# Graph network on one core: 48 slots for gathered tiles in four passes, and edge results stored by pairs of groups

## The reference, cut to what matters

```
# block 0, three layers
f = einsum(x @ fc_w[l].T + fc_b[l], norm_out, ch_w[l])
agg = segment_sum(f[src] * edge_w, dst)          # a weighted sum
# block 1
out = segment_max(relu(theta(x[dst] - x[src]) + phi(x[src])), dst)
# block 2: attention over edges and self loops
# block 3, three layers
e = relu((x[dst] - x[src]) @ thetas[l].T + x[src] @ phis[l].T)
agg = segment_max(e, src); batch norm; relu
```

## Time and profile before

| what | value |
|---|---|
| median of 3 executions | 4967.33 us |
| the profiled execution's own time | 4953.19 us |
| its span, first to last instruction | 4951.5 us |
| POOL busy | 3314.2 us (67%), 3435 instructions |
| DVE busy | 3038.7 us (61%), 9035 instructions |
| PE busy | 1527.9 us (31%) |
| ACT busy | 1032.0 us (21%) |
| gathers of line 1287 | 2744, busy 1510.6 us and 1146.0 us |
| stores of line 1270 | 686 of 512 KB, 3.2 us to landing |
| mean DMA rate | 181 GB/s |

### The profile page before, as it was taken

One profiled execution on the slowest core, in us unless ns is written; L12 is line 12 of the kernel. 1 busy time (PEld: TensorE's weight loads), 2 busy tenths in 40 slices (PEclk: granted clock), 3 DMA queues, 4 the chain that ended last, 5 costly groups with the idle time before them and its releaser, 6 DMA issues. The chain is left out here.

```text
span 4951.5 us, 34938 instructions
## 1 busy us (share of the span) xinstructions
PE 1527.9 (31%) x7148; PEld 1041.6 (21%) x7148; DVE 3038.7 (61%) x9035; ACT 1032.0 (21%) x2614; POOL 3314.2 (67%) x3435
## 2 busy tenths in 40 slices
PE   6221075556655565445520001400006000330004
PEld 5110053334433343112320001300005000230003
DVE  5897565556656568999868888633334333433335
ACT  3333334443344432000121111200002000110002
POOL 3777747776577755777657774177775777657774
PEclk8555575555655578875665555755558555665556
DMA  2766636665466634666446664166654666456663
GB/s 86 230 195 222 209 122 207 209 206 178 149 210 206 210 106 134 205 204 205 150 131 222 218 220 141 59 205 205 206 191 138 204 204 206 152 177 204 204 207 118
DMA packets 319655, 898.09 MB, mean 181 GB/s; under 512 B 75371, under 2 KB 111576, under 8 KB 319320
## 3 DMA queue, kind: packets, MB, share of 16 engines
q0 software_dynamic: 161760, 439.40, 31.9%
q1 hardware_dynamic: 157688, 456.53, 24.7%
HBM read 449.86 MB, written 445.80 MB: 181 GB/s over the span
## 5 line engine op out<-in xcount | busy, mean ns | idle before, releaser
L1287 POOL DMA_INDIRECT WORK<-table,SRCI x1568 | 1510.6, 963 | 640.0 <-issue 512.9
L1287 POOL DMA_INDIRECT WORK<-table,BYSRC x1176 | 1146.0, 975 | 559.1 <-issue 435.5
L1336 DVE SCALAR_TENSOR_TENSOR WORK<-WORK,LOWE 128x256 f32<-128x256 f32 x1564 | 763.3, 488 | 964.7 <-DMA WORK<-table,BYSRC 892.8
L1336 DVE SCALAR_TENSOR_TENSOR WORK<-WORK,NST,e_mv 128x256 f32<-128x256 f32 x1173 | 563.2, 480 | 499.7 <-ACT e_mv L1306 261.0
L1306 ACT ACTIVATE e_mv<-WORK,WE 128x256 f32<-128x256 f32 x1176 | 491.3, 463 | 826.7 <-DMA WORK<-table,SRCI 788.1
L990 PE MATMUL bn_ps<-ident,WORK 128*128 128x128 f32 x6 | 2.0, 434 | 1490.0 <-PEq L148 1490.0
L1641 POOL DMA_INDIRECT WORK<-table_attention,SRCI x392 | 373.5, 953 | 119.4 <-issue 118.8
L990 PEld LDWEIGHTS bn_ps<-ident,WORK 128*128 128x128 f32 x6 | 0.9, 203 | 1491.1 <-issue 1491.1
L1418 ACT ACTIVATE WORK<-bn_ps 128x256 f32<-128x256 f32 x3 | 1.2, 384 | 1495.2 <-PE bn_ps L1001 1495.2
L961 PE MATMUL e_hi<-ARENA 128*128 128x392 bf16 x392 | 185.1, 472 | 262.4 <-DVE ARENA L947 262.4
L897 PE MATMUL e_rb<-ARENA 98*128 98x128 bf16 x392 | 114.7, 293 | 443.5 <-ACT ARENA L913 443.5
(11 more groups left out here) (355 smaller groups left out, 4379.9 us busy)
## 6 DMA issues: line engine op xcount, KB each, us to landing
edge_results<-WORK SPq DMA_DIRECT2D x686, 512.0 KB, 3.2
edge_results_attention<-WORK SPq DMA_DIRECT2D x98, 544.0 KB, 3.2
WORK<-table,SRCI POOLq DMA_INDIRECT x1568, 2.9
table<-ARENA SPq DMA_DIRECT2D x35, 640.0 KB, 3.2
WORK<-table,BYSRC POOLq DMA_INDIRECT x1176, 2.9
WORK<-table_attention,SRCI POOLq DMA_INDIRECT x392, 3.2
table_attention<-ARENA SPq DMA_DIRECT2D x5, 660.0 KB, 3.4
X<-in_x SPq DMA_DIRECT2D x4, 640.0 KB
```

The lines of the kernel that those rows point to most:

```text
L1287: eng.indirect_dma_start(G[:, q * GT + k, 0:D], None, T, bass.IndirectOffsetOnAxis(ap=index[:, t:t + 1], axis=0)).then_inc(got[q].sem, 16)
L1336: eng.scalar_tensor_tensor(O[:, q % OB, k, :], behind, mask[:, ds(g * GT + k, 1)], here, op0, op1).then_inc(linked, 1)
```

## The change

It does two things in `edge_pass`.

1. In the four passes for a maximum (e3, e5, e6, e7) there are twelve sets of four slots in place of six, 48 in all. The new 24 lie in `AGW_BASE`. POOL there waits, before the gathers of group g, for group g - 12 in place of g - 6. Twelve semaphores count landed gathers in place of six. The weighted passes keep 24 slots.
2. In all seven passes SP stores after every odd group only, two groups (8 KB from every partition, 1024 KB) at once. There are 343 stores in place of 686. The ring of four groups stays; DVE waits before every even group g for the store of groups g - 4 and g - 3, which is issued after group g - 3. At the end SP waits for two counts in place of four.

```diff
--- before.py
+++ after.py
@@ -21,6 +21,7 @@
 GT = 4
 NG = -(-E // (P * GT))
 SETS = 6
+DEEP = 2 * SETS
 ET = NG * GT
 EP = ET * P
 CHAIN = ET
@@ -152,7 +153,7 @@
     top = ExitStack()
     Stage.used = []
     with top:
-        gathered = [Gathered(top.enter_context(nc.semaphore(f"gathered_{k}"))) for k in range(SETS)]
+        gathered = [Gathered(top.enter_context(nc.semaphore(f"gathered_{k}"))) for k in range(DEEP)]
         def sb(name, shape, dt=F32):
             return top.enter_context(nc.sbuf_tensor(name, shape, dt))
 
@@ -1249,10 +1250,18 @@
         def edge_pass(name, index, ops, mask, weighted, beside=nothing_beside):
 
             op0, op1 = ops
-            U = 2 * SETS
+            sets = SETS if weighted else DEEP
+            U = 2 * sets
+            more, = carve(AGW_BASE, ((SETS * GT, D), F32))
+
+            def slot(g, k):
+
+                at = g % sets * GT + k
+                return G[:, at, 0:D] if at < SETS * GT else more[:, at - SETS * GT, :]
+
             with Stage(nc, name) as st:
-                got = gathered
-                stored = [st.sem(f"stored{b}") for b in range(OB)]
+                got = gathered[0:sets]
+                stored = [st.sem(f"stored{b}") for b in range(OB // 2)]
                 moved, linked = (st.sem(n) for n in ("moved", "linked"))
                 mv = st.stack.enter_context(nc.psum_tensor(f"{name}_mv", [P, 4, 2 * D], F32))
                 side = beside(st, name)
@@ -1266,25 +1275,28 @@
                 @block.sync
                 def _(eng):
                     def store(g, q, turn):
-                        eng.wait_ge(linked, g * GT + (GT + 8))
-                        eng.dma_start(PRC[:, ds(g * GT, GT), :], O[:, q % OB, :, :]).then_inc(stored[q % OB], 16)
+
+                        if g % 2:
+                            eng.wait_ge(linked, g * GT + (GT + 8))
+                            pair = O[:, g % OB - 1:g % OB + 1, :, :].rearrange("p g k d -> p (g k) d")
+                            eng.dma_start(PRC[:, (g - 1) * GT:(g + 1) * GT, :], pair).then_inc(stored[g % OB // 2], 16)
 
                     early, late = beside_on("sync", eng)
                     pipelined(NG, U, eng, *early, (store, 0), *late, flat=flat)
-                    for b in range(OB):
-                        eng.wait_ge(stored[b], 16 * -(-(NG - b) // OB))
+                    for b in range(OB // 2):
+                        eng.wait_ge(stored[b], 16 * -(-(NG // 2 - b) // (OB // 2)))
 
                 @block.gpsimd
                 def _(eng):
                     for g in range(NG):
-                        q = g % SETS
-                        if g >= SETS and weighted:
-                            eng.wait_ge(moved, 2 * (g - SETS + 1))
-                        elif g >= SETS:
-                            eng.wait_ge(linked, GT * (g - SETS + 1) + 8)
+                        q = g % sets
+                        if g >= sets and weighted:
+                            eng.wait_ge(moved, 2 * (g - sets + 1))
+                        elif g >= sets:
+                            eng.wait_ge(linked, GT * (g - sets + 1) + 8)
                         for k in range(GT):
                             t = g * GT + k
-                            eng.indirect_dma_start(G[:, q * GT + k, 0:D], None, T,
+                            eng.indirect_dma_start(slot(g, k), None, T,
                                                    bass.IndirectOffsetOnAxis(ap=index[:, t:t + 1], axis=0)).then_inc(got[q].sem, 16)
 
                 @block.tensor
@@ -1298,12 +1310,12 @@
                 @block.scalar
                 def _(eng):
                     def move(g, q, turn):
-                        got[q % SETS].arrived(eng, turn * (U // SETS * GT) + (q // SETS * GT + GT))
+                        got[g % sets].arrived(eng, g // sets * GT + GT)
                         for h in range(2):
                             eng.wait_ge(linked, g * GT + (2 * h + 2))
-                            bank, first = mv[:, 2 * (q % 2) + h, :], q % SETS * GT + 2 * h
+                            bank = mv[:, 2 * (q % 2) + h, :]
                             for k in range(2):
-                                last = eng.activation(bank[:, k * D:(k + 1) * D], G[:, first + k, 0:D], ACT.Copy,
+                                last = eng.activation(bank[:, k * D:(k + 1) * D], slot(g, 2 * h + k), ACT.Copy,
                                                       scale=WE[:, ds(g * GT + (2 * h + k), 1)])
                             last.then_inc(moved, 1)
 
@@ -1318,12 +1330,12 @@
 
                     def link(g, q, turn):
                         for k in range(GT):
-                            if k == 0 and not (isinstance(g, int) and g < OB):
-                                eng.wait_ge(stored[q % OB], turn * (U // OB * 16) + q // OB * 16)
+                            if k == 0 and g >= OB and g % 2 == 0:
+                                eng.wait_ge(stored[g % OB // 2], g // OB * 16)
                             if not weighted:
                                 if k == 0:
-                                    got[q % SETS].arrived(eng, turn * (U // SETS * GT) + (q // SETS * GT + GT))
-                                here = G[:, q % SETS * GT + k, 0:D]
+                                    got[g % sets].arrived(eng, g // sets * GT + GT)
+                                here = slot(g, k)
                             else:
                                 if k % 2 == 0:
                                     eng.wait_ge(moved, g * 2 + (k // 2 + 1))
@@ -1339,8 +1351,8 @@
                     pipelined(NG, U, eng, *early, (link, 0), *late, flat=flat, head=0 if flat else U)
                     if "vector_end" in side:
                         side["vector_end"](eng)
-            for q in range(SETS):
-                got[q].close(GT * ((NG - q + SETS - 1) // SETS))
+            for q in range(sets):
+                got[q].close(GT * ((NG - q + sets - 1) // sets))
 
 
         YT = YBASE[:, 0:2 * NP].rearrange("p (k n) -> p k n", k=2)
@@ -1602,7 +1614,7 @@
 
             U = SETS
             with Stage(nc, "att") as st:
-                got = gathered
+                got = gathered[0:SETS]
                 stored = [st.sem(f"stored{b}") for b in range(OB)]
                 names = ("raw_in", "first", "er_in", "flags_in", "masks", "packed", "chain", "scored", "expd", "dens", "rowed", "weighed", "linked",
                          "dens_in", "rescaled", "made")
```

## The result

The changed kernel takes 4955.33 us in the median of 20 runs against 4963.78 us of the kernel before in as many; the ratio is 0.9985, with an interval of 0.9979 to 0.999. The medians lie 8.5 us apart; by the ratio it is faster by 7 us, some 5 to 10. The profiled execution's span is 4946.3 us, from 4951.5.

What follows compares the result with a forecast made beforehand. POOL's issuing of 392 gathers was taken to bound each pass. Ends +7, phase in the last three passes -15, e1 and e2 -8 make -16 us, from the 4967.3 median to 4951 us; range 4922 to 4988.

Steps and rivals of the forecast that it cites:

- e3: Pass for a maximum, held by DVE itself; an odd group can't begin much sooner: 0, within 5 us either way.
- e6: Pass for a maximum: the store's phase was to save 5 us, with the mean gather at 0.960 to 0.965 us.
- What bounds the kernel: Each of seven passes is as long as POOL's issuing of its 392 gathers; DVE and SP only follow.
- the signs of being wrong: Mean gather of the last three passes staying above 0.970 us, or DVE waiting for stores.
- Part 1: 48 slots: POOL is released earlier only where it waits for a slot; gain 0, bounds 0 and 4.3 us.
- The phase in e5 to e7: Store disturbs every second group only; a pair pays 0.145 instead of 0.245 us: -15 us, bounds -36 and 0.
- the first tooth: Gather starting 0.11 us into DVE's links is lengthened by 0.245 us, falling one for one to nothing at 0.36.
- The ends: Last store of each pass is on the path: 10.0 us lost, 2.9 back from sooner last links, +7 us.
- e1 and e2: Line 263 after odd groups' links comes 0.26 us sooner and misses the gather: -8 us, bounds 0 and -11.
- e0: Store's phase in this weighted pass: 0.
- The sum: 7 - 15 - 8 = -16 us on the median of 4967.3: 4951 us, -0.3%, chance 0.50.
- The sharing of SBUF: Skill's rule on two-input DVE instructions fits lengthened gathers; by its descriptor inference phase is free and only +7 stays.

Runs made afterwards that it cites:

- the slots alone: Against the kernel before: 48 slots in four passes for a maximum, still one store a group; ratio 1.0007 (0.9998 to 1.0016).
- the split pair: Against the changed kernel: each pair goes as two 512 KB stores back to back, 24 slots; 4947.47 us, ratio 0.9979 to the kernel before.
- The PSUM kernel: Against the kernel before: ACT first copies each tile to PSUM in four passes for a maximum, for DVE's links; 4906.51 us, ratio 0.9907; repeated, 0.9905.
- the pairs alone: Against the kernel before: pair stores in all seven passes, 24 slots everywhere; ratio 0.9982 (0.9973 to 0.9991).

## Why the prediction was right in its direction and half right in its sum

**What bounds the kernel** held: POOL's gathers fill every pass, before and after. Of the signs of being wrong neither came: the mean gather of e5 to e7 is 0.961 to 0.967 us, under 0.970, and DVE waited for no store. **Part 1** held: 0 for the slots, shown by the slots alone.

**The phase in e5 to e7** held, and the size nearly: -5 us a pass forecast, -5.0, -3.7 and -3.6 measured in the excess, 12 in place of 15 (and 15 without the 0.003 us that every gather of this profile has on top). The odd group's links begin at 2.8 as forecast from the earlier trace rows. The even group's were put between 3.6 and 4.1 and came at 4.7. The whole pair pays 0.12 to 0.17 us, by luck about the 0.145 taken: the even group's links take 0.10 of it, but from other gathers than forecast, the one at 5.00 under the first tooth and the one at 6.25 under the fourth; the odd group's take 0.03, where 0 was forecast; the rest is the 0.003 us on every gather. The step that was off is that the 1024 KB store would delay a gather no more than a 512 KB one does. The delay grows with the data: 2.8 with no store, 3.6 to 3.9 with 512 KB, 4.7 with 1024 KB, in one store or two, and 1024 KB take 1.24 us more to flow. It isn't that the pair's store is issued earlier against the gather: 15 last gathers in e5 to e7 of the kernel before have their 512 KB store issued from 0.3 us before to 0.1 after their start, as most pairs are, and there the links begin 3.7 us after the gather in the median. The delay is some two thirds of the store's own flow: 0.9 of 1.43 us, and 1.9 of 2.67. The Trainium skill (DMA: Bandwidth & Descriptors, Queues, rings and completion order) has each engine change between queues only after a whole packet, of some 9 to 17 descriptors. If a store is one such packet for each engine, a gather behind it waits for all of it, and the growth from 3.7 to 4.7 agrees; but then two stores would delay it no more than one, and the split pair's 4.7 does not agree. How the stores are packed no run shows.

**The ends** were wrong: "The last store is on the path", +7. In e5 to e7 it was POOL, 8.80 us after its last gather in both kernels, and the longer store fitted into the slack. In e0 to e2 the slack was shorter, 0.6 to 0.8 us, and the stage starts moved by 0.3 to 0.4 us each from the last gather's end. That is about 1 us in place of 7; the sooner last links, for which 2.9 were given back, decide nothing either while POOL arrives last. What was left out was to line up the stage's start with POOL's last instruction in several passes; the equal 8.8 would have shown.

**e1 and e2** were wrong: -8 forecast, 1.7 found. Links and line 263 (264 in the changed kernel) did come 0.3 us sooner after an odd group's last gather, 3.7 in place of 4.0, as forecast. But the gather then met the second of the two one-hot instructions, of which the forecast said that it cost nothing:

```profile
935.26 2.10 DVE L1348 SCALAR_TENSOR_TENSOR WORK<-WORK,NST,e_mv 128x256 f32<-128x256 f32 x4 [1.57 <-ACT e_mv L1318]
...
937.27 0.76 DVE L264 TENSOR_TENSOR ARENA<-ARENA,iota_b 128x392 bf16<-128x392 bf16 x2
...
937.81 1.04 POOL L1299 DMA_INDIRECT WORK<-table,SRCI  x1 [0.31 <-issue]
```

It starts 0.54 after line 264 begins and takes 1.04, where the one of the earlier trace rows started 0.27 after and took 1.11. (The second instruction runs from 937.75 to 938.03.) The tooth of the second instruction was not looked for; it is lower, because the instruction is half as long. What line 263 costs went from 5.8 and 5.9 us to 3.8 and 4.2.

**e3** was wrong by more than its bounds: 0 within 5, and +8.3 found. The argument that DVE's one-hots pace it and so nothing moves missed that the even group's landing, 1 us later, throws DVE behind: then the two alternating states, which happened to be cheap there, dissolve. In the kernel before the links begin 3.8 and 3.55 us after the last gather, within 0.05, group after group; in the changed one anywhere from 3.8 to 5.1 and 3.1 to 4.8 (the middle eight tenths). Both sorts of instruction cost more for it: the links 14.0 us after 8.2, the one-hots 6.4 after 4.6. The PSUM kernel bears it out: there pairs cost e3 2 us, not 8. That the pairs did it is shown by e3 at 503 us without them.

**e0**: 0 forecast, +2 in this profile. It is hardly the pairs' phase against the links. 1.1 us is the 0.003 us on every gather, and 1.0 is in the three longest gathers, 2.64, 1.77 and 1.12 us instead of 1.59, 1.57 and 1.33, which meet DVE's set-up work and not its links. A gather of 2.6 us stands there in the kernels with single stores too.

**The sum.** The seven passes with their ends give -2 us, the whole span -5.2, and the runs -7 (-5 to -10). Some 3 us of the span lie in stretches that the change doesn't touch (the first gather starts 1.4 us sooner). With the pairs alone the gap is wider: 1 us less in the seven windows, a span of 4951.7 us, and 9 us by the runs. A single profiled execution differs from another by as much: the stretch from e3's last gather to e5's first took 781 to 794 us in these profiles. In the changed kernel's profile the 0.003 us on each of POOL's 3136 gathers also hides some 9 us; whether its other executions have it no run shows. So where the rest of the 7 us comes from stays open.

**The sharing of SBUF.** The sentence of the Trainium skill that spoke for collisions (SBUF — State Buffer, Who interferes with whom: two SBUF inputs on DVE against a GpSimd instruction that reads SBUF) agrees with this trace, down to 0.1 to 0.3 us a pass once one input is in PSUM. Its inference that such an instruction does not hinder descriptor generation these runs leave open: a gather also reads its index column from SBUF, and which part of it waits no run separates. The section has the later of the two blocked until the earlier is done, and here too the trace agrees. The sawtooth is a wait for the end of the DVE instruction: 437 of the 457 lengthened gathers of the kernel before end 0.82 us after a DVE instruction has ended, whatever its length. e0 of the changed kernel has the longest case:

```profile
250.80 2.64 POOL L1299 DMA_INDIRECT WORK<-table,SRCI  x1 [0.31 <-issue]
250.86 1.75 DVE L752 TENSOR_TENSOR ARENA<-ARENA 128x1536 f32<-128x1536 f32 x1
```

The instruction ends at 252.62 by the trace, and the gather, 0.82 later, at 253.44. (It started 0.06 before this instruction, which follows the one ahead without a gap; in e5 to e7, where 0.035 us lie between links, no gather that starts before a link is held by it.) A tooth is no higher than 0.26 us in e5 to e7 only because a link is no longer than 0.485 us.

## What to carry to other kernels

Look for the engine whose instructions fill the time, and then at the spread of their durations: 2% on 2744 gathers were worth 45 us here, and it hung on the operands of another engine's instructions. A gather that meets one waits for its end, so a long instruction of this kind costs more than a short one. A change of phase (fewer, larger or later stores) moves such collisions about, gains in one pass and loses in the next; putting one operand in PSUM removes them. More buffers for an engine that never waits for one buy nothing, and before the last store is called the end of a stage, see which engine arrives last there.

## What the runs showed of the hardware that was not expected

- A gather that meets a DVE instruction with two SBUF operands ends 0.82 us after that instruction's end, instead of 0.945 after its own start. It meets a link if it starts more than 0.09 us after it. So its lengthening is a sawtooth of its start, up to 0.26 us for a link of 0.485 us and 1.7 us for an instruction of 1.75. For the links it is gone when one operand is in PSUM. Line 945, which reads one tensor and a column, lengthens gathers in the same way.
- A gather that starts within 0.09 us of a link's start is not lengthened; the link then takes 0.51 us in the mean, and up to 0.55, instead of 0.485.
- The landing of a 128 KB gather issued right behind a store goes from 2.8 us (to the first use) to 3.6 to 3.9 behind 512 KB and 4.6 to 4.8 behind 1024 KB, whether that is one store or two.
- POOL passes the end of a block 8.6 us after its last gather has ended, in all seven passes of the kernel before, and nothing in the timeline shows what it does in that time.
- A store of 8 KB from each partition flows at 390 GB/s in packets of 8 KB, one of 4 KB at 367 GB/s.
